# Token tiles moved by lists of row numbers, and router logits in four pieces

## The reference

```python
x = x + 0.5 * ffn(layernorm(x))     # mixture of experts, then the same again at the end
x = x + attention(layernorm(x))     # 16 heads of 64, causal
x = x + 0.5 * ffn(layernorm(x))

def ffn(h):                          # gate_w is 64 x 128
    scores = sigmoid(h @ gate_w.T)   # the router logits are h @ gate_w.T
    # bias, best 4 of 8 groups, best 8 of 64 experts, weights normalised to sum 2.5
    y = sum over 64 experts of weight[e] * ((silu(h @ Wg[e]) * (h @ Wu[e])) @ Wd[e])
    return y + silu(h @ Sg) * (h @ Su) @ Sd
```

## Time and profile before

| | |
|---|---|
| median of 3 runs | 1957.73 us (1955.67 to 1958.81) |
| span of the profiled execution, first to last instruction | 1954.6 us |
| PE (TensorE) busy | 1800.7 us, 92% |
| DVE (VectorE) busy | 1625.8 us, 83% |
| ACT (ScalarE) busy | 1096.4 us, 56% |
| POOL (GpSimd) busy | 809.4 us, 41% |
| DMA queue q1 | 149.08 MB, 34.8% of 16 engines |

### The profile page before, as it was taken

How to read it: one execution, slowest core, us unless ns; L and a number is a source line. 1 busy time by engine, 2 the same in 40 slices (tenths; PEclk the granted TensorE clock), 3 DMA queues, 4 the chain that set the end, 5 groups by cost and what they waited for, 6 DMA issues and landing times. The chain is left out here.

```text
span 1954.6 us, 32354 instructions
## 1 busy us (share of the span) xinstructions
PE 1800.7 (92%) x9065; PEld 1355.3 (69%) x9065; DVE 1625.8 (83%) x3273; ACT 1096.4 (56%) x2568; POOL 809.4 (41%) x612
## 2 busy tenths in 40 slices
PE   5798989989899989999999999979989999899998
PEld 3566767667676767777777777756767667676676
DVE  6899898998989867777777777768898988989887
ACT  3554545545455556666666666744545545554554
POOL 2465655656566710000000000015656656566566
PEclk8999999999999999999999999989999999999999
DMA  7954544445444400000000000023545545454453
GB/s 162 179 120 97 118 94 106 110 90 118 98 107 110 108 1 1 0 0 0 0 0 0 0 0 0 1 65 89 117 102 111 113 97 115 100 111 110 103 121 86
DMA packets 109534, 149.63 MB, mean 77 GB/s; under 512 B 30128, under 2 KB 43056, under 8 KB 109488
## 3 DMA queue, kind: packets, MB, share of 16 engines
q1 hardware_dynamic: 109488, 149.08, 34.8%
HBM read 144.87 MB, written 4.19 MB: 76 GB/s over the span
## 5 line engine op out<-in xcount | busy, mean ns | idle before, releaser
L764 POOL TENSOR_TENSOR f_hid_lo<-f_hid,f_hid_hi 128x512 fp32r<-128x512 f32 x528 | 767.1, 1466 | 597.1 <-ACT f_hid_hi L586 596.1
L586 ACT CAST f_hid_hi<-f_hid 128x512 fp32r<-128x512 f32 x528 | 326.8, 619 | 431.9 <-DVE f_hid L658 431.5
L658 DVE TENSOR_TENSOR f_hid<-f_mix_wide,f_hid 128x512 f32<-128x512 f32 x512 | 540.5, 1056 | 29.4 <-DMA f_mix_wide<-mix_rows 15.6
L647 DVE TENSOR_TENSOR f_hid<-bank,f_hid 128x512 f32<-128x512 f32 x528 | 359.3, 681 | 109.4 <-ACT f_hid L577 57.8
L577 ACT ACTIVATE f_hid<-bank 128x512 f32<-128x512 f32 x528 | 315.6, 598 | 191.7 <-PE bank L479 163.3
L477 PE MATMUL bank<-f_hid_hi,wd_hi 128*128 128x512 f32 x528 | 228.4, 433 | 90.6 <-POOL f_hid_lo L764 89.6
L477 PEld LDWEIGHTS bank<-f_hid_hi,wd_hi 128*128 128x128 f32 x528 | 99.1, 188 | 186.9 <-POOL f_hid_lo L764 171.6
L921 POOL TENSOR_TENSOR n_veps<-n_moments,eps 128x2 f32<-128x2 f32 x16 | 3.6, 224 | 517.4 <-DVE n_moments L900 517.4
L477 PE MATMUL bank<-r_xT_hi,wg_hi 128*128 (+1 forms) x528 | 216.3, 410 | 1.5 <-PEq L954 1.5
L477 PE MATMUL bank<-r_xT_hi,wu_hi 128*128 (+1 forms) x528 | 210.4, 399 | 0.0
L478 PE MATMUL bank<-r_xT_hi,wg_lo 128*128 (+1 forms) x528 | 210.4, 398 | 0.0
(11 more groups left out here) (167 smaller groups left out, 3151.5 us busy)
## 6 DMA issues: line engine op xcount, KB each, us to landing
f_mix_wide<-mix_rows SPq DMA_DIRECT2D x252, 512.0 KB, 6.5
landing<-in_L_ffn_We_gate SPq DMA_DIRECT2D x4, 512.0 KB, 9.0
landing<-in_L_ffn_We_up SPq DMA_DIRECT2D x4, 512.0 KB, 8.2
landing<-in_L_ffn_We_down SPq DMA_DIRECT2D x4, 512.0 KB, 6.9
mix_rows<-r_mixT SPq DMA_DIRECT2D x32, 64.0 KB, 2.1
out<-x_all SPq DMA_DIRECT2D x8, 256.0 KB, 6.8
f_mix_wide<-mix_rows SPq DMA_DIRECT2D x4, 384.0 KB, 5.4
f_mix_wide<-mix_rows SPq DMA_DIRECT2D x4, 128.0 KB, 2.9
```

The costliest lines, as they stand in the source:

```text
L586: nc.scalar.copy(hid_hi[:, p % 3, :], hid[:, p % 3, :]).then_inc(hid_hi_done, 1)
L647: nc.vector.tensor_tensor(hid[:, p % 3, :], up_bank[p % 3][:, :], hid[:, p % 3, :], ALU.mult)\
L658: nc.vector.tensor_tensor(hid[:, p % 3, :], mix_wide[:, g % 2, p % SPREAD, :], hid[:, p % 3, :], ALU.mult).then_inc(weighted, 1)
L764: nc.gpsimd.tensor_tensor(hid_lo[:, p % 3, :], hid[:, p % 3, :], hid_hi[:, p % 3, :].bitcast(F32), ALU.subtract).then_inc(hid_lo_done, 1)
```

## The change

Three things are changed.

Eight of the 28 later tiles of x (tiles 4 to 11) are no longer in SP's transfer. GpSimd first writes a table of row numbers with `iota` (column t of partition p holds 128 t + p), waits for it, and then issues eight indirect transfers, each of 128 rows of 512 bytes, in the middle of its constants. VectorE waits for these and for the smaller transfer before it takes the moments of chunk 1.

The last chunk's four tiles are written by four indirect transfers of GpSimd in place of one transfer of SP. SP waits for both kinds at the end.

The router logits are computed in four pieces of 128 columns, each a sum of three matmuls: twelve matmuls in place of three, over the same columns.

```diff
@@ constants
+GATHERED = 8
@@ def logits(n), on TensorE
             pe.wait_ge(xT_lo_done, n + 1)
-            for a, (wk, xt) in enumerate((("gw_hi", xT_hi), ("gw_lo", xT_hi), ("gw_hi", xT_lo))):
-                mm = nc.tensor.matmul(misc[:, :], w[wk][:, :], xt[:, half(n, CHUNK)],
-                                      start=(a == 0), stop=(a == 2))
+            xh, xl = xT_hi[:, half(n, CHUNK)], xT_lo[:, half(n, CHUNK)]
+            for j in range(CT):
+                t = slice(j * P, (j + 1) * P)
+                nc.tensor.matmul(misc[:, t], w["gw_hi"][:, :], xh[:, t], start=True, stop=False)
+                nc.tensor.matmul(misc[:, t], w["gw_lo"][:, :], xh[:, t], start=False, stop=False)
+                mm = nc.tensor.matmul(misc[:, t], w["gw_hi"][:, :], xl[:, t], start=False, stop=True)
             mm.then_inc(logits_done, 1)
@@ VectorE, slot MOMENTS of chunk 0 of the first layer
+                            dve.wait_ge(x_gathered, 16 * GATHERED)
                             dve.wait_ge(x_rest, 16)
@@ GpSimd, other_constants(), after the memsets of the padding, before those of mask and ident_b
+                nc.gpsimd.iota(w["row_no"][:, :], [[P, w["row_no"].shape[1]]], base=0, channel_multiplier=1)\
+                    .then_inc(rows_numbered, 1)
+                pool.wait_ge(rows_numbered, 1)
+                for t in range(CT, CT + GATHERED):
+                    nc.gpsimd.indirect_dma_start(x_all[:, t, :], None, x_rows[:, :],
+                                                 bass.IndirectOffsetOnAxis(ap=w["row_no"][:, t:t + 1], axis=0))\
+                        .then_inc(x_gathered, 16)
@@ GpSimd, second layer, after its last slot
+            if out is not None:
+                pool.wait_ge(x_updated, NC)
+                for t in range(CT * (NC - 1), CT * NC):
+                    nc.gpsimd.indirect_dma_start(out[1][:, :],
+                                                 bass.IndirectOffsetOnAxis(ap=w["row_no"][:, t:t + 1], axis=0),
+                                                 x_all[:, t, :], None).then_inc(scattered, 16)
@@ SP, chunk 0 of the first layer, after spread group 1
-                            sp.dma_start(x_all[:, CT:, :], x[:, CT:, :]).then_inc(x_rest, 16)
+                            sp.dma_start(x_all[:, CT + GATHERED:, :], x[:, CT + GATHERED:, :])\
+                                .then_inc(x_rest, 16)
@@ SP, end of the second layer
             if out is not None:
-                store_x(NC - 1)
-                sp.wait_ge(stored, 16 * NC)
+                sp.wait_ge(stored, 16 * (NC - 1))
+                sp.wait_ge(scattered, 16 * CT)
@@ macaron
+    x_flat = x.rearrange("b m d -> (b m) d")
+    out_flat = out.rearrange("b m d -> (b m) d")
+        w["row_no"] = sb("row_no", [P, tiles], U32)
```

More of the change, by code:

```diff
@@ L27 @@
 BF16 = mybir.dt.bfloat16
+U32 = mybir.dt.uint32
 ALU = mybir.AluOpType
@@ L404, in ffn @@
         first_spread = sem("first_spread")
-        stored = sem("stored")
+        stored, scattered = sem("stored"), sem("scattered")
         if load:
-            x, dr = load
+            x, x_flat, dr = load
             pieces = weight_pieces(w, dr)
@@ L412, in ffn @@
             landed = [sem(f"landed{n}") for n in range(len(pieces))]
-            x_first, x_rest, gw_landed, bias_landed, po_landed = (
-                sem(n) for n in ("x_first", "x_rest", "gw_landed", "bias_landed", "po_landed"))
+            x_first, x_gathered, x_rest, gw_landed, bias_landed, po_landed = (
+                sem(n) for n in ("x_first", "x_gathered", "x_rest", "gw_landed", "bias_landed", "po_landed"))
             hi_split, lo_split, gw_turned, gw_split = sem("hi_split"), sem("lo_split"), sem("gw_turned"), sem("gw_split")
@@ L418, in ffn @@
                 sem(n) for n in ("const_step", "ident_ready", "earlier_ready", "padded", "wd_padded"))
+            rows_numbered = sem("rows_numbered")
+            x_rows = x_flat
         GROUPS = PAIRS // SPREAD
@@ L807, in store_x @@
                 sp.wait_ge(x_updated, c + 1)
-                sp.dma_start(out[:, tiles(c), :], x_all[:, tiles(c), :]).then_inc(stored, 16)
+                sp.dma_start(out[0][:, tiles(c), :], x_all[:, tiles(c), :]).then_inc(stored, 16)
             def piece(n):
@@ L1402, in macaron @@
         rows = row_norm(ctx, nc, w, x_all)
-        ffn(nc, "f1_", w, x_all, psum, mix_rows, b, first, rows=rows, load=(x_v, dr))
+        ffn(nc, "f1_", w, x_all, psum, mix_rows, b, first, rows=rows, load=(x_v, x_flat, dr))
         attention(nc, w, x_all, psum, rows, second)
-        ffn(nc, "f2_", w, x_all, psum, mix_rows, b, second, out=out_v)
+        ffn(nc, "f2_", w, x_all, psum, mix_rows, b, second, out=(out_v, out_flat))
 _INS = ["L0_attn_x", "L0_attn_P_q", "L0_attn_P_k", "L0_attn_P_v", "L0_attn_P_o", "L0_ffn_gate_w", "L0_ffn_gate_bias",
```

## The result

The changed kernel takes 1961.14 us (median of 18 runs, 1959.59 to 1963.67); the kernel before, run beside it on the same chip, 1957.74 us (18 runs, 1955.13 to 1959.46). The ratio is 1.0019, 95% interval 1.0013 to 1.0026: slower by 3.4 us, just inside the 0.2% taken as the bound. 1961.4 us had been predicted, and a range of 1957.0 to 1967.5. The profiled execution has a span of 1958.1 us, 3.5 above that of before.

What follows compares the result with a forecast made beforehand. TensorE and VectorE were taken to alternate as the limit, with no cover at start, saturated transfers and end. Terms 0.6 + 0.6 + 0 - 2.2 + 4.7 = +3.7 us gave 1961.4 us, range 1957.0 to 1967.5.

Steps and rivals of the forecast that it cites:

- The step of 0.11 us: Router logits on TensorE: one 128-column matmul to the next takes 0.11 us at full clock, 0.23 at half.
- Rival 3: Logits everywhere: narrow fp32r matmuls cost as much as wide ones, +13.0 us, 1970.7 us in all; chance 0.08.
- The start, 0.6: Kernel start at 1.2 GHz, serial chain: narrow logits make the sigmoid 0.6 us later (bounds 0 and +2.8).
- Rival 4: Kernel start: GpSimd's lists hold up VectorE's routing steps, +2.6 us, 1964.0 us in all; chance 0.10.
- Attention, 0.6: Logits in attention, close to bound by TensorE: the added 0.6 us comes through in full (bounds 0 and 2.1).
- The slots, 0: 14 places in expert layers: TensorE's added 0.62 us is taken from waits of 1.09 in sum, cost 0.
- shorter by 0.6 in sum: Steady chunk: TensorE's waits at the down matmuls after the logits shrink by 0.6 us, period still 82.1.
- The gathers, 0: Start: eight GpSimd gathers hide in its 25.9 us of idle time before 34.68, cost 0.
- The relief, -2.2: SP's full queue loses 0.524 MB; VectorE's 6.38 us wait for routing weights shortens by 2.2 us (bounds 0 and 4.3).
- rival 2: SP's full queue: the relief is larger, -4.3 us in place of -2.2, 1959.3 us in all; chance 0.17.
- The end, +4.7: After the last update: four GpSimd scatters at 1.28 us plus 1.9 to landing, 7.0 us for 2.3 (bounds +1.2, +8.4).
- Rival 1: End: scatters are dear, deciding from 1.33 us each; at 2.20 us, end +8.4, whole +7.4, 1965.1 us; chance 0.22.

Runs made afterwards that it cites:

- e6_gather_spare: Kernel before plus the eight gathers, landing in a routing-weight buffer not yet in use, SP still bringing all 28 tiles; 1956.49 us against 1957.12, ratio 0.9999.
- e4_early8: Kernel before with the same eight tiles moved early by a plain SP transfer and SP's later one cut to 20; 1950.66 us against 1953.32, ratio 0.9986.
- e3_gather: Kernel before with only the eight GpSimd gathers and SP's transfer cut to 20 tiles, wide logits, no scatter; 1952.95 us against 1953.32, ratio 0.9997.
- e11_plain4: Kernel with the four scatters alone, but four plain GpSimd transfers in place of the lists; 1956.13 us against the kernel before's 1955.82, ratio 1.0003.
- e1_logits: Kernel before with only the logits in twelve 128-column matmuls; 1955.0 us against 1953.32, ratio 1.0004.
- e2b_scatter: Kernel before with only row numbers and the four scatters at the end, second timing of that kernel; 1959.31 us against 1955.82, ratio 1.0020.
- e0_before: The kernel before, unchanged, timed against itself as if it were another; ratio 0.9997.
- e5_early28: Kernel before with all 28 later tiles of x brought early by SP, none behind the routing weights; 1951.55 us against 1957.12, ratio 0.9968.
- e8_scatter2: Kernel before with two of the last four tiles stored by GpSimd's lists, two by one SP transfer; 1956.32 us against 1955.82, ratio 1.0006.
- e10_iota: Kernel before with only the row numbers added (buffer, iota and its wait), no GpSimd transfer; ratio 0.9999.

## Why the prediction held, point by point

**The step of 0.11 us.** Right: the logits lie 0.11 us apart at the full clock (twelve in 1576.26 to 1577.55 = 1.29 us, 1.32 expected), and 0.216 at the start where 0.23 had been taken. Rival 3, narrow matmuls at the price of wide ones, is out.

**The start, 0.6.** Right, with 0.5 for the logits. How early the start's first transposes begin differs by trace (7.39 to 7.82 us), so the distance from them to the sigmoid is what counts: 4.94 us in both traces of before, 5.44 in the changed kernel, 5.45 with the logits alone, 8.00 with 24 matmuls. The sigmoid at 13.26 in place of 12.55 is these 0.5 us, and 0.2 of chance ahead of the logits. The first r_mix is at 25.54 where before has 24.73 and 24.91. Rival 4, VectorE held up by the lists, is out: from the sigmoid to the first r_mix it is 12.2 us before and 12.3 after, and e6_gather_spare has the first r_mix +0.3 us later at most.

**Attention, 0.6.** Right: 0.66 to 0.67, from update to update it takes 38.15 us before, 38.81 with the logits alone, and 1261.77 - 1222.95 = 38.82 in the changed kernel.

**The slots, 0.** Right, and with more cover than the prediction counted. It said that 1.09 us of waiting stood against 0.62; but the first wait alone takes the 0.62, and behind the second there are more, so that 1.94 us are hidden as well. Its sign "shorter by 0.6 in sum" came out as 0.5.

**The gathers, 0.** Right, by e6_gather_spare. The lists took 10.9 us, 10.2 had been taken (eight of 1.28).

**The relief, -2.2.** The mechanism is right: the bytes leave the full queue and VectorE's wait shortens, 6.38 to 3.33 where 4.2 was expected. What it is worth is less sure. The transfer of the rest lands 2.0 us sooner in the mean (12.9 against 14.9 us), which is close to bytes over bandwidth; the wait loses 3.1 in the mean (3.15 against 6.25). From r_mix to r_mix the three kernels with eight tiles early take 85.3 us in the mean against 88.7: -3.4; the changed kernel's own 86.0 is -2.7. Timed, e4_early8 gives -2.7 and e3_gather -0.6, each with 1.8 either side. So 2.2 lies among them, and the term was probably low, by 0.5 to 1.2; rival 2, with its 4.3, is as far off on the other side. With 28 tiles timing and r_mix agree, at 6.3; there the wait of 6.3 us is used up, which caps it below the 7.6 of bytes over bandwidth. Why eight tiles should give over half of what 28 give, as by r_mix they do, stays open.

**The end, +4.7.** Right in kind, 0.6 too high: a step is 1.26 us where 1.28 had been taken. That it hit is luck, since the 1.28 is an operation on data, and e11_plain4 shows that 128 rows without a list take 0.59. The rest is in the landing, 2.2 us from the start of the last list, which had been put at 1.28 + 1.9. Only 0.3 us of delay between the update and the first list work against it. +4.1 in the changed kernel, +4.2 in both runs of the scatters alone. Rival 1, which wanted over 1.33 us for each scatter, is out, by 0.07 us a step.

**The sum.** By rows: 0.5 (start) + 0.67 - 2.7 (the changed kernel's own relief) + 4.1 = +2.6, or +1.9 with the mean relief of 3.4. By timed parts: 0.8 (e1_logits) - 0.6 (e3_gather) + 3.9 (e2b_scatter) = +4.1, each with some 1.8 either side. Measured: +3.4 by the medians, 2.5 to 5.1 by the ratio's interval. That the forecast's +3.7 came so near is partly luck: by rows the relief was taken too small and the end 0.6 too high, both in the same direction, and what is measured lies 0.8 to 1.5 above the sum by rows. In the one profiled execution of the changed kernel 1.7 us went to attention's start (below) and 1.8 came back by three fewer long periods; had every execution lost the 1.7, the sum by rows would be 3.6 to 4.3. For the median of 18 runs no row says what makes up the difference, and it is within what the parts can tell.

## What to carry to other kernels

At the end of a kernel nothing hides an engine's issue time: hand the last store to the queue that issues it in one instruction, and keep GpSimd's lists (1.26 us for 128 rows, and serial) for places where the engine is idle and nobody waits. Before moving a load to another engine, try to issue it earlier on the same one: here the gain of the gathers was in the moment at which the bytes moved, and one transfer on SP that brings all of x early gained 6 us where the change lost 3. Where an engine waits many times a little for another that holds the limit, the cover of an added operation is not the nearest wait alone but the next ones too, one after another, until the added time is used up.

## What the runs showed of the hardware that was not expected

- The third gather took 1.96 us, the others 0.94 to 1.18. VectorE was working on two operations of 128x1024 elements (10.53 to 12.90) meanwhile; the same list was slow in e3_gather (1.98) and in e6_gather_spare (1.97). VectorE's operations kept their 1.22 us. It looks as if lists can wait for a wide VectorE operation, and not the other way round; no run varied it. The Trainium skill's rule (the same section as above) has this direction; its size, 3100 ns for 620, is not seen: here it was 1.0 us more.
- At the start of attention the granted clock falls for some us in nine of the fourteen traces, and not in the other five. The windows of the changed kernel and of e0_before there:

```profile
703.00:709.00 6.00, 5.24 (x19) 3.70 (x20) 3.14 (x12) 2.40 (x5) 0.89 (x2) 0.72 0.00 1
```
```profile
697.00:709.00 12.00, 10.17 (x58) 7.27 (x59) 8.30 (x25) 7.60 (x23) 0.90 (x2) 1.00 0.00 1
```

  It costs the changed kernel's trace 1.7 us of what it had gained by then (its updates of x ran 3.3 us ahead of before's, and 1.5 us after it). Over 680 to 720 us the nine have a granted clock of 0.87 to 0.96 in the mean, the five of 1.00: both of before, e5_early28, e8_scatter2 and e11_plain4. From the last update of the first layer to the first of attention these five take 51.7 to 51.8 us, the nine 52.0 (e4_early8) to 55.0 (e3_gather). Narrow logits are not needed for it, since e3_gather, e4_early8 and e10_iota have wide ones, and GpSimd's transfers are in kernels of both sorts. Two kernels have two traces each, and these agree (none in before, a fall in both of the scatters alone). Yet it is hardly in every execution of a kernel: the traces of e1_logits and e6_gather_spare lose 2.2 and 2.3 us here against those five, and the kernels are timed at +0.8 and -0.2 us. What decides it was not tested.
- What makes a chunk 81.5 or 82.1 us long stands in the traces at one place, 33.6 us behind the update of x, where a low part of GpSimd and VectorE's multiplication by routing weights start within 0.01 us of each other. In before, a chunk of 81.5 us and then one of 82.1:

```profile
1513.57 1.83 POOL L764 TENSOR_TENSOR f_hid_lo<-f_hid,f_hid_hi 128x512 fp32r<-128x512 f32 x1 [1.38 <-ACT f_hid_hi L586]
1513.58 0.69 DVE L658 TENSOR_TENSOR f_hid<-f_mix_wide,f_hid 128x512 f32<-128x512 f32 x1
```
```profile
1595.08 1.29 POOL L764 TENSOR_TENSOR f_hid_lo<-f_hid,f_hid_hi 128x512 fp32r<-128x512 f32 x1 [1.38 <-ACT f_hid_hi L586]
1595.09 1.83 DVE L658 TENSOR_TENSOR f_hid<-f_mix_wide,f_hid 128x512 f32<-128x512 f32 x1
```

  Either VectorE takes 0.69 us and GpSimd 1.83, or GpSimd 1.29 and VectorE 1.83: one runs and the other is held up. So it is in all 154 steady chunks of the fourteen traces, the second way in the 41 long ones and the first way in the 113 short ones. GpSimd's start is recorded 4 to 10 ns ahead of VectorE's in the long ones and 0 to 6 ns in the short ones, so which way it goes hangs on a few nanoseconds, which these starts barely tell apart, and is worth 0.6 us. No run moved one of the two on purpose.
